# AdaLN transformer block: LN2's turned rows and three weight sets split in high and low fp32r parts; query and key buffers for three head groups instead of four

## The chip, the cores and the metric

The kernel is one launch on one core of one Trainium2 chip. The metric is the time of the whole launch in device microseconds. Before the change the median of three runs is 1087.39 us (1085.41 to 1090.95). The engines are TensorE (PE; its weight loads are a row of their own, PEld), VectorE (DVE), ScalarE (ACT), GpSimd (POOL) and SyncE (SP), which here only issues transfers.

## The reference, cut to what matters

Batch 4, 1024 tokens, width 256, 16 heads of 16. An attention block is followed by a block with eight small autoencoders, of which the one with the least error picks an adapter for the batch.

```python
mod = (silu(c) @ wmod).reshape(4, 6, 1, 256)           # sa, ca, ga, sb, cb, gb; |ga|, |gb| at least 0.25
h = layernorm(x) * (1 + ca) + sa
q, k, v = split_heads(h @ qkv_w.T)                      # 16 heads of 16
x = x + ga * (softmax(q @ k.T / 4) @ v @ proj_w.T + proj_b)

h = layernorm(x) * (1 + cb) + sb                        # "LN2"; below: h2
base = h @ W_base + b_base                              # 256 x 256
hid  = relu(h @ W_enc[n] + b_enc[n])                    # n = 0..7, 256 x 64 each: together 256 x 512
recon = hid @ W_dec[n] + b_dec[n]
top1 = argmin_n mean((recon - h) ** 2)                  # one adapter for a batch of the block
mid  = relu(h @ W_down[top1] + b_down[top1])            # 256 x 64
x = x + gb * (base + mid @ W_up[top1] + b_up[top1])     # 64 x 256
```

All inputs and outputs are float32. (The FFN part of the reference names 16 batches of 256 tokens as its shape constants; with the arrays that come in, it runs on 4 batches of 1024.)

## The kernel before, in words

**Units.** The attention is cut into 256 units. A head group `gi` (0 to 15) is four heads of one batch; with a half `c` of 512 queries it makes a pass, 32 in all, in the order of the table `SEQ`. A pass has 8 units, one for each 128 keys. A unit is four score products `E` (one for each head; PE writes 128 keys x 512 queries in a bank `pE`, ACT takes its exponential into `P`, L1003), and one `PV`, which multiplies `P` with V into `pO`. The row maximum is needed first: `M` (1024 products, 32 for each pass) computes scores the other way round into `pM`, and DVE reduces them (L1124). The maxima are turned (`mturn`) and sent by DMA into two extra rows of the query operand `QO`. M runs at least 48 products ahead of E.

Both have room for four groups. A copy of group `gi` waits until the last E of group `gi - 4` has been read. `hi` and `lo` are one buffer: a group's ACT step waits until the group before has landed.

**The rest, for each batch.** `proj` (attention output), `bn2`, `ln2s`, `ln2n` (LN2's statistics and normalised rows X), `xturn` (PE turns X; ACT scales it into `h2T`, features on partitions, with the sum over tokens, L1086), `xsq` (ACT squares `h2T`, L1095), `enc` (8 tiles of 128 tokens x 512, each two fp32 products over halves of the 256 features; DVE takes the maximum into `Hb`, L1279), `gram` (`half` in the last batch), `pick`, `select` and `fetch` (the chosen adapter's weights come by four DMAs), `base` or, in batches 0 to 2, the base product inside `out`, `mid`, `out`. `prepb` on POOL scales W_base by gb into `wbg`.

**What sets the order.** `order()` writes one list of steps, and each engine runs its own part of it in that order. `plan()` gives due units; `before(s)` gives the steps that must lie some units back. A burst is 3 E and about 3 M, and then either one or two PV, or pieces of long steps; QUIET steps (work of ACT, DVE and POOL) and SHORT steps (transposes) follow a burst. When all M are out (unit 243), E goes on alone, with pieces between. After the last PV, the second half of the last batch's LN2, `enc`, `half`, `pick`, `select`, `fetch`, `base`, `mid` and `out` run one behind the other. PE waits for a bank before it writes in it: three `pM`, three `pE` and one `pX`.

L701 is the helper `mm`: all products with weights other than transposes have this line.

## Time and profile before

| | |
|---|---|
| median of 3 runs | 1087.39 us |
| profiled execution | 1087.94 us |
| its span | 1086.1 us |
| outside the span | 1.84 us |
| mean granted TensorE clock | 0.974 |
| PE, DVE, ACT, POOL busy | 95%, 73%, 59%, 17% |

A PE row of a product covers its fill and drain too, so that rows overlap and 95% busy isn't 95% of PE's peak. What a product costs is read from the distance between the starts of successive weight loads or products. An fp32 product appears as two records, an fp32r product as one. PEclk is the granted clock of TensorE as a share of its higher level. Rows of POOL are rough.

### The profile page before, as it was taken

Reading aid. Unit: us, or ns where it says so; the run is one execution under the profiler, and the core shown is the slowest. Engines: PE = TensorE matmul, PEld = TensorE weight load, DVE = VectorE, ACT = ScalarE, POOL = GpSimd, SP = SyncE. Lnnn points to the kernel's source line nnn. Section 1 sums busy time; section 2 is a strip of 40 time slices with the busy share of each in tenths; the row PEclk is TensorE's granted clock in tenths of the full one; section 3 lists DMA queues with packets and bytes.
Section 4 is the critical chain, followed back from the end, with each engine's and each line's share of the span. In section 5 each row is a group of like instructions: output and inputs, shape, how many; then the busy total and the mean of one; then the engine's idle time right before and its main releaser. Section 6 shows DMA issues by size and latency. Waiting matters only on the chain.

```text
span 1086.1 us, 15998 instructions
## 1 busy us (share of the span) xinstructions
PE 1032.0 (95%) x5824; PEld 496.9 (46%) x5824; DVE 795.4 (73%) x1565; ACT 644.1 (59%) x1261; POOL 180.3 (17%) x300
## 2 busy tenths in 40 slices
...
PEclk7979999999999999998999999999999998999988
...
GB/s 162 181 1 70 2 79 25 64 76 25 69 1 70 20 41 20 59 26 59 97 11 69 13 10 59 20 44 118 84 35 2 1 2 26 49 49 3 1 1 44
DMA packets 33218, 48.60 MB, mean 45 GB/s; under 512 B 6947, under 2 KB 25384, under 8 KB 33132
## 3 DMA queue, kind: packets, MB, share of 16 engines
...
## 4 chain that ended last, share of the span: by engine, by line
PE 85%; DVE 7%; ACT 5%; issue 2%; DMA 1%; SPq 0%; POOL 0%; ACTq 0%; DVEq 0%
PE pE L701 26%; PE pX L701 23%; PE pO L701 22%; PE pM L701 11%; DVE mx L1124 2%; ACT P L1003 1%; ACT h1T L1037 1%; ACT h2T L1086 1%; ACT hi L1053 1%; PE pX L760 1%; DVE Atok L1149 1%; DVE lo L1212 1%; DVE Hb L1279 1%; PE pX L826 0%; DVE junk L1263 0%
## 5 line engine op out<-in xcount | busy, mean ns | idle before, releaser
L1124 DVE TENSOR_REDUCE mx<-pM 128x1 f32<-128x512 f32 x1006 | 630.1, 681 | 117.7 <-PE pM L701 115.1
L1003 ACT ACTIVATE P<-pE 128x512 f32<-128x512 f32 x995 | 525.6, 599 | 245.2 <-PE pE L701 242.1
L701 PE MATMUL pM<-KO,QO 48*128 48x512 f32 x1006 | 368.8, 454 | 6.1 <-DVE mx L1124 3.7
L701 PE MATMUL pE<-QO,KO 50*128 50x512 f32 x995 | 349.1, 440 | 20.7 <-DVE Atok L1149 7.4
L701 PEld LDWEIGHTS pE<-QO,KO 50*128 50x128 f32 x995 | 164.2, 187 | 241.2 <-issue 134.6
L701 PE MATMUL pO<-P,V 128*17 128x512 f32 x2048 | 258.7, 603 | 1.0 <-ACT P L1003 1.0
L701 PEld LDWEIGHTS pM<-KO,QO 48*128 48x128 f32 x1006 | 163.8, 187 | 35.7 <-DVE mx L1124 23.9
L1442 POOL CAST mh<-mxc 128x16 fp32r<-128x16 f32 x32 | 6.4, 202 | 502.4 <-DVE mxc L1133 502.3
L701 PEld LDWEIGHTS pO<-P,V 128*17 128x17 f32 x2048 | 41.5, 96 | 102.8 <-issue 94.6
L701 PE MATMUL pX<-h1T,wqkv_s 128*128 128x512 f32 x112 | 60.9, 648 | 0.6
L701 PE MATMUL pX<-X,Hb 128*128 128x258 f32 x208 | 53.4, 395 | 0.7 <-DVE lo L1212 0.7
L701 PEld LDWEIGHTS pX<-X,Hb 128*128 128x128 f32 x208 | 37.0, 190 | 14.8 <-issue 8.9
L701 PE MATMUL pX<-wenc_s,h2T 128*128 128x512 f32 x72 | 39.6, 654 | 1.6 <-ACT h2T L1086 1.4
L1212 DVE SCALAR_TENSOR_TENSOR lo<-pX,cst,hi 128x512 fp32r<-128x512 f32 x28 | 21.0, 751 | 26.7 <-ACT hi L1053 26.6
L701 PE MATMUL pX<-Hb 128*128 128x128 f32 x224 | 31.6, 289 | 0.0
L701 PEld LDWEIGHTS pX<-Hb 128*128 128x128 f32 x224 | 28.9, 199 | 5.8 <-issue 5.2
L1053 ACT ACTIVATE hi<-pX,cst 128x512 fp32r<-128x512 f32 x28 | 19.2, 686 | 17.8 <-PE pX L701 17.5
L1501 POOL TENSOR_SCALAR X<-x,mv,rs 128x256 f32<-128x256 f32 x24 | 29.2, 1226 | 1.5 <-POOL rs L1491 0.5
L1406 POOL TENSOR_SCALAR xin<-xin,mv,rs 128x256 f32<-128x256 f32 x24 | 29.2, 1224 | 1.0
L701 PEld LDWEIGHTS pX<-h1T,wqkv_s 128*128 128x128 f32 x112 | 18.3, 193 | 20.6 <-issue 17.1
L1010 ACT ACTIVATE osb<-pO 128x512 f32<-128x512 f32 x32 | 19.2, 600 | 12.9 <-PE pO L701 12.6
L701 PE MATMUL pE<-wenc_s,h2T 128*128 128x512 f32 x52 | 24.3, 592 | 0.0
...
## 6 DMA issues: line engine op xcount, KB each, us to landing
KO<-hi SPq DMA_DIRECT2D x56, 128.0 KB, 4.0
QO<-hi SPq DMA_DIRECT2D x56, 128.0 KB, 5.8
...
KO<-lo SPq DMA_DIRECT2D x28, 128.0 KB, 3.8
QO<-lo SPq DMA_DIRECT2D x28, 128.0 KB, 6.3
...
```

The source lines that it names most:

```text
L701: return e.matmul(o, lhsT, rhs, start=start, stop=stop)
L760: a = e.transpose(o[:, 128 * k:128 * k + 128], osb[:, 128 * k:128 * k + 128], ident)
L1003: e.activation(P[:, u % 3, j, :], bank(s), ACT.Exp).then_inc(*empties(s))
L1010: e.activation(osb[:, :], pO[:, :], ACT.Copy).then_inc(s_osb, 1)
L1037: a = e.activation(h1T[:, c, 256 * k:256 * k + 256], bank(s)[:, 256 * c:256 * c + 256], ACT.Identity, bias=modT[:, c, b:b + 1], scale=modT ...
L1053: e.activation(halves(gi)[0][:, cs], bank(s), ACT.Identity, scale=qscale).then_inc(s_hi, 1)
L1086: e.activation(h2T[:, c, 512 * th:512 * th + 512], bank(s), ACT.Identity, bias=modT2[:, c, b:b + 1], scale=modT2[:, 2 + c, b:b + 1], accum ...
L1124: e.tensor_reduce(mx[:, hq % 2, k:k + 1, kh], bank(s), AX.X, ALU.max, negate=True).then_inc(*empties(s))
L1149: e.tensor_tensor(dst, v[:, :, :, 0:HD], rec[:, :, :].unsqueeze(3).to_broadcast([128, 4, 4, HD]), ALU.mult).then_inc(*empties(s))
L1212: e.scalar_tensor_tensor(out=lo_[:, cs], in0=bank(s), scalar=qscale, in1=hi_[:, cs].bitcast(F), op0=ALU.mult, op1=ALU.subtract).then_inc(* ...
L1406: a = e.tensor_scalar(xt[:, t, :], xt[:, t, :], mv1[:, k, t, 0:1], rs1[:, k, 1, t:t + 1], ALU.subtract, ALU.mult)
L1501: a = e.tensor_scalar(X[:, t, 0:D], x2[:, t, :], mv2[:, t, 0:1], rs2[:, 1, t:t + 1], ALU.subtract, ALU.mult)
```

## The change

1. `h2T` is gone. `xturn` writes into a buffer `h2f` with room for half the tokens; a new step `xhi` writes the high part `h2h` (ACT, a copy) and the low part `h2l` (POOL, a subtraction), both fp32r. In the last batch's second half both are done by DVE.
2. W_enc is split once by POOL into `weh` and `wel` (`wsplit`, unit 24); `wbg` for each batch into `wbh` and `wbl` (`prepb`); the chosen W_down into `wdh` and `wdl` (`fetch`: POOL, in the last batch DVE).
3. Each fp32 product in `enc`, `base`, the base part of `out`, and `mid` becomes three fp32r products (`thrice`): high x high, high x low, low x high.
4. To have room for this, `QO` and `KO` hold three groups instead of four. A copy of group `gi` waits for the last E of group `gi - 3`, and in the list it isn't put before that unit is over. The due units of `qk` move, `SEQ` takes the two halves of queries apart for the last three groups only, and the last batch's first half is due 7 units later.
5. `h2f` shares memory with W_enc as it is loaded, and the unsplit `wbg` with the squares of `xsq` (`junkx`), from which waits follow (`s_wen`, `s_wbg`, `s_xsq`, `s_hl`). `mid` waits for the split W_down alone and no longer for all four DMAs.

```diff
-SEQ = [(gi, c) for gi in range(4 * NB - 4) for c in range(2)]
-SEQ += [(4 * NB - 4 + g, c) for c in range(2) for g in range(4)]
+SEQ = [(gi, c) for gi in range(4 * NB - 3) for c in range(2)]
+SEQ += [(4 * NB - 3 + g, c) for c in range(2) for g in range(3)]
...
+    at(24, ("wsplit", 0), ("wsplit", 1))
     for gi in range(2, 4 * NB):
-        u = {2: 0, 3: 8, 13: 168, 14: 177, 15: 188}.get(gi, 16 * gi - 36)
+        u = {2: 0, 4 * NB - 1: 200}.get(gi, 16 * gi - 34)
...
-            halves = ((B - 30, (0, 1)), (B, (2, 3))) if q == LAST else ((B, (0, 1, 2, 3)),)
+            halves = ((B - 23, (0, 1)), (B, (2, 3))) if q == LAST else ((B, (0, 1, 2, 3)),)
...
-        return [(("ln1turn", b, 2 * a[1] + i), 1) for i in range(2)] + (
-            [(("qk", gi // 4, gi % 4, 1), 7)] if gi > 1 else [])
+        return [(("ln1turn", b, 2 * a[1] + i), 1) for i in range(2)] + [(("moved", 4 * b + a[0] - 1), 2)]
...
+            [(("xhi", b, a[0] - 2), 0), (("xsq", b, 0), 0)] if a[0] > 1 else [])
+    if kind == "xhi":
+        return [(("xturn", b, a[0]), 0.7)]
...
-        return [(("xturn", b, 2 * (a[0] // 4) + i), 1) for i in range(2)]
+        return [(("xhi", b, 2 * (a[0] // 4) + i), 1.5) for i in range(2)]
...
-        for _ in range(3):
-            if moving:
+        for _ in range(6 if moving and moving[0][1] == 4 * NB - 1 else 3):
+
+            if moving and (moving[0][1] < 3 or at >= 32 * (SEQ.index((moving[0][1] - 3, 1)) + 1)):
                 out.append(moving.popleft())
...
-        QO = sb("QO", [128, 2, 4, T], R)
-        KO = sb("KO", [128, 2, 4, T], R)
+        QO = sb("QO", [128, 3, 2, T], R)
+        KO = sb("KO", [128, 3, 2, T], R)
...
+        def split(b, k):
+
+            return (s_hL, k - 1) if b == LAST and k > 1 else (s_hl, 4 * b + k + 1)
+
+        def thrice(mm, o, xh, xl, wh, wl, start, stop):
+
+            mm(o, xh, wh, start, False)
+            mm(o, xh, wl, False, False)
+            return mm(o, xl, wh, False, stop)
...
-                        pe.wait_ge(d_w[6], 16)
+                        pe.wait_ge(s_wen, 2)
                         for c_ in range(2):
-                            pe.wait_ge(*emptied("xturn", b, 2 * (t // 4) + c_))
-                    a = mm(o, h2T[:, c, 128 * t:128 * t + 128], wenc_s[:, c, :], c == 0, c == 1)
+                            pe.wait_ge(*split(b, 2 * (t // 4) + c_))
+                    sl = slice(128 * t, 128 * t + 128)
+                    a = thrice(mm, o, h2h[:, c, sl], h2l[:, c, sl], weh[:, c, :], wel[:, c, :], c == 0, c == 1)
...
-                        pe.wait_ge(d_sel, 64 * (b + 1))
-                    a = mm(o[0:H, :], wdn[:, c, :], h2T[:, c, 512 * h:512 * h + 512], c == 0, c == 1)
+                        pe.wait_ge(*((s_wdL, 1) if b == LAST else (s_wdn, b + 1)))
+                    sl = slice(512 * h, 512 * h + 512)
+                    a = thrice(mm, o[0:H, :], wdh[:, c, :], wdl[:, c, :], h2h[:, c, sl], h2l[:, c, sl], c == 0, c == 1)
...
                         for c in range(2):
-                            mm(r, h2T[:, c, 128 * tt:128 * tt + 128], wbg[:, c, :], c == 0, False)
+                            thrice(mm, r, h2h[:, c, sl], h2l[:, c, sl], wbh[:, c, :], wbl[:, c, :], c == 0, False)
...
+                elif kind == "xhi" and not (s[1] == LAST and s[2] > 1):
+                    act.wait_ge(*(full("out", b - 1, 3) if b else landed(1)))
+                    act.wait_ge(*emptied("xturn", b, k))
+                    e.activation(h2h[:, c, 512 * th:512 * th + 512], h2f[:, c, :], ACT.Copy).then_inc(s_hh, 1)
...
+                elif kind == "xhi" and s[1] == LAST and s[2] > 1:
+                    e.tensor_copy(h2h[:, c, sl], h2f[:, c, :]).then_inc(*link.up())
+                    dve.wait_ge(*link.now())
+                    e.tensor_tensor(h2l[:, c, sl], h2f[:, c, :], h2h[:, c, sl].bitcast(F), ALU.subtract).then_inc(s_hL, 1)
+
+                elif s == ("fetch", LAST):
+                    dve.wait_ge(d_wdn, 16 * NB)
+                    e.tensor_copy(wdh[:, :, :], wdn[:, :, :]).then_inc(*link.up())
+                    dve.wait_ge(*link.now())
+                    e.tensor_tensor(wdl[:, :, :], wdn[:, :, :], wdh[:, :, :].bitcast(F), ALU.subtract).then_inc(s_wdL, 1)
...
+                elif kind == "xhi" and not (s[1] == LAST and s[2] > 1):
+                    pool.wait_ge(s_hh, nth[s])
+                    e.tensor_tensor(h2l[:, c, sl], h2f[:, c, :], h2h[:, c, sl].bitcast(F), ALU.subtract).then_inc(s_hl, 1)
...
-                    if gi >= 4:
-
-                        sp.wait_ge(*full("E", 8 * SEQ.index((gi - 4, 1)) + 7, 3))
+                    if gi >= 3:
+
+                        sp.wait_ge(*full("E", 8 * SEQ.index((gi - 3, 1)) + 7, 3))
```

**PE, behind the last PV: the second half of the last batch.** `cst,X` are the transposes of `xturn`, `X,Hb` belongs to `half`. Before:

```order
L859 MATMUL pE<-cst,X 128x128 [waits XL,free3]
L859 MATMUL pE<-cst,X 128x128 x3
L859 MATMUL pM<-cst,X 128x128 x4
L701 MATMUL pX<-wenc_s,h2T 128x512 [waits free1,free3]
L701 MATMUL pX<-wenc_s,h2T 128x512
L701 MATMUL pM<-wenc_s,h2T 128x512 x2
L701 MATMUL pE<-wenc_s,h2T 128x512 [waits free5]
```

PE at the same place, now:

```order
L886 MATMUL pE<-cst,X 128x128 [waits XL,free4]
L886 MATMUL pE<-cst,X 128x128 x3
L886 MATMUL pM<-cst,X 128x128 x4
L728 MATMUL pX<-weh,h2h 128x512 [waits hL]
L728 MATMUL pX<-wel,h2h 128x512
L728 MATMUL pX<-weh,h2l 128x512
L728 MATMUL pX<-weh,h2h 128x512
L728 MATMUL pX<-wel,h2h 128x512
L728 MATMUL pX<-weh,h2l 128x512
```

The order of the steps is the same; two products of a tile have become six, and the first waits for DVE's low part (`hL`) instead of ACT's write.

**DVE at that place,** where `junk,accA` ends the `half` before and `Hb` takes the `enc` results. Before:

```order
L1289 ISA accA 128x1
L1279 TENSOR_TENSOR Hb<-pX,nbe 128x512 [waits full6,free0]
L1279 TENSOR_TENSOR Hb<-pM,nbe 128x512 [waits full2]
L1279 TENSOR_TENSOR Hb<-pE,nbe 128x512 [waits full5]
L1279 TENSOR_TENSOR Hb<-pE,nbe 128x512 [waits full4]
```

DVE there, now:

```order
L1327 ISA accA 128x1
L1361 CAST h2h<-h2f 128x512 [waits free4,free2]
L1363 TENSOR_TENSOR h2l<-h2f,h2h 128x512 [waits vlink]
L1361 CAST h2h<-h2f 128x512 [waits free0]
L1363 TENSOR_TENSOR h2l<-h2f,h2h 128x512 [waits vlink]
L1317 TENSOR_TENSOR Hb<-pX,nbe 128x512 [waits full6]
```

Two casts and two subtractions have come in ahead of the first `Hb`.

**ACT in batch 1,** at the first two `xturn` (`P` is the exponential of E). Before:

```order
L1086 ACTIVATE h2T,xbar<-pX,modT 128x512 [waits full6,full2]
L1086 ACTIVATE h2T,xbar<-pE,modT 128x512 [waits full5]
L1003 ACTIVATE P<-pE 128x512 [waits full3]
L1003 ACTIVATE P<-pE 128x512 [waits full4]
L1003 ACTIVATE P<-pE 128x512 [waits full5]
L1003 ACTIVATE P<-pE 128x512 [waits full3]
```

ACT there, now:

```order
L1116 ACTIVATE h2f,xbar<-pX,modT 128x512 [waits full6,hl]
L1116 ACTIVATE h2f,xbar<-pE,modT 128x512 [waits full4,hl]
L1033 ACTIVATE P<-pE 128x512 [waits full5]
L1033 ACTIVATE P<-pE 128x512 [waits full3]
L1033 ACTIVATE P<-pE 128x512 [waits full4]
L1125 ACTIVATE h2h<-h2f 128x512 [waits free6]
L1125 ACTIVATE h2h<-h2f 128x512 [waits free4]
L1033 ACTIVATE P<-pE 128x512 [waits full5]
```

Two copies stand one burst behind the two writes of `h2f`, and these wait for POOL's low parts of the buffer's last content (`hl`).

**SP, the last group's copies.** `QO<-mT` are the maxima of a pass. In the list before, group 15's copies stand ahead of batch 2's last output stores and input loads:

```order
L1570 DMA KO<-hi 16x2x1024 [waits full4,free6]
L1570 DMA KO<-lo 16x2x1024
L1570 DMA KO<-hi 16x2x1024 x2
L1570 DMA KO<-lo 16x2x1024
L1570 DMA KO<-hi 16x2x1024
L1570 DMA QO<-hi 16x2x1024 x2
L1570 DMA QO<-lo 16x2x1024
L1570 DMA QO<-hi 16x2x1024 x2
L1570 DMA QO<-lo 16x2x1024
L1630 DMA out<-x 128x2x256 [waits free6]
```

SP there, now:

```order
L1662 DMA QO<-mT 2x4x128 [waits free2]
L1662 DMA QO<-mT 2x4x128 x3
L1653 DMA KO<-hi 16x2x1024 [waits full5,free6]
L1653 DMA KO<-lo 16x2x1024
L1653 DMA KO<-hi 16x2x1024 x2
L1653 DMA KO<-lo 16x2x1024
L1653 DMA KO<-hi 16x2x1024
L1653 DMA QO<-hi 16x2x1024 x2
L1653 DMA QO<-lo 16x2x1024
L1653 DMA QO<-hi 16x2x1024 x2
L1653 DMA QO<-lo 16x2x1024
L1662 DMA QO<-mT 2x4x128 [waits free3]
```

They stand in units 208 and 209 now, behind the maxima of pass 26, and nothing but maxima follows. The first M of group 15 stands at the start of unit 212.

## Rows read from the trace of the kernel before

**Rows 1.** The page, part 1 and the granted clock of part 2.
```profile
PE 1032.0 (95%) x5824; PEld 496.9 (46%) x5824; DVE 795.4 (73%) x1565; ACT 644.1 (59%) x1261; POOL 180.3 (17%) x300
PEclk7979999999999999998999999999999998999988
```

**Rows 2.** The page, part 4: the chain that ended last.
```profile
PE 85%; DVE 7%; ACT 5%; issue 2%; DMA 1%; SPq 0%; POOL 0%; ACTq 0%; DVEq 0%
```

**Rows 3.** Windows of 40 us: length, busy us by engine, clock, DMA.
```profile
80.00:120.00 40.00, 39.78 (x231) 15.90 (x234) 36.73 (x66) 31.65 (x63) 4.54 (x10) 1.00 0.33 48
...
320.00:360.00 40.00, 38.19 (x196) 15.18 (x192) 31.13 (x58) 25.05 (x50) 8.49 (x13) 1.00 0.31 53
```

**Rows 4.** PE's groups by form: busy us, mean ns, idle before.
```profile
L701 PE MATMUL pM<-KO,QO 48*128 48x512 f32 x1006 | 368.8, 454 | 6.1 <-DVE mx L1124 3.7 <-DVE h2T L1212 1.1 <-ACT h2T L1086 0.5
L701 PE MATMUL pE<-wenc_s,h2T 128*128 128x512 f32 x52 | 24.3, 592 | 0.0
```

**Rows 5.** PE's weight loads in order of time: start, us, load.
```profile
1050.36 0.19 PEld L701 LDWEIGHTS pM<-wenc_s,h2T 128*128 128x128 f32 x1 [0.24 <-issue]
1050.79 0.19 PEld L701 LDWEIGHTS pM<-wenc_s,h2T 128*128 128x128 f32 x1 [0.24 <-issue]
...
1056.09 1.61 PEld L701 LDWEIGHTS pM<-X,Hb 128*128 128x128 f32 x8 [1.67 <-issue]
1057.72 1.07 PEld L701 LDWEIGHTS pM<-Hb 128*128 128x128 f32 x8
1058.72 1.39 PEld L701 LDWEIGHTS pE<-X,Hb 128*128 128x128 f32 x7
```

**Rows 6.** The burst at 829 us, in order of time.
```profile
828.11 0.50 PE L701 MATMUL pE<-QO,KO 50*128 50x512 f32 x1
828.71 1.57 ACT L1003 ACTIVATE P<-pE 128x512 f32<-128x512 f32 x3 [1.45 <-PE pE L701]
828.75 1.89 DVE L1124 TENSOR_REDUCE mx<-pM 128x1 f32<-128x512 f32 x3 [1.47 <-PE pM L701]
829.01 0.30 PEld L701 LDWEIGHTS pX<-wenc_s,h2T 128*128 128x128 f32 x2 [0.37 <-issue]
...
831.78 0.18 PEld L701 LDWEIGHTS pE<-QO,KO 50*128 50x128 f32 x1 [0.76 <-issue]
```

**Rows 7.** Groups by form on ACT, POOL and DVE.
```profile
L1010 ACT ACTIVATE osb<-pO 128x512 f32<-128x512 f32 x32 | 19.2, 600 | 12.9 <-PE pO L701 12.6
...
L1470 POOL TENSOR_TENSOR wbg<-wb_s,bc 128x512 f32<-128x512 f32 x4 | 5.2, 1291 | 0.0
...
L1279 DVE TENSOR_TENSOR Hb<-pX,nbe 128x512 f32<-128x512 f32 x18 | 12.3, 685 | 14.6 <-PE pX L701 14.6
```

**Rows 8.** A one-input DVE pass over 128x512 in SBUF, in order of time.
```profile
71.71 0.41 DVE L1250 TENSOR_SCALAR nbe<-nbe 128x512 f32<-128x512 f32 x1
```

**Rows 9.** The end of the last batch, in order of time.
```profile
1045.62 0.77 ACT L1086 ACTIVATE h2T<-pM,modT 128x512 f32<-128x512 f32 x1
...
1046.62 3.47 PE L701 MATMUL pX<-wenc_s,h2T 128*128 128x512 f32 x4 [1.37 <-ACT h2T L1086]
...
1075.46 1.90 PE L701 MATMUL pM<-h2T,wdn 128*64 128x512 f32 x4 [1.08 <-DMA wug<-in_bup]
...
1079.01 1.13 PE L701 MATMUL pM<-wug,mid 65*128 65x256 f32 x4
```

**Rows 10.** POOL behind the maxima of passes 26 and 27.
```profile
827.34 0.20 POOL L1442 CAST mh<-mxc 128x16 fp32r<-128x16 f32 x1 [10.06 <-DVE mxc L1133]
...
861.19 0.20 POOL L1442 CAST mh<-mxc 128x16 fp32r<-128x16 f32 x1 [33.20 <-DVE mxc L1133]
```

**Rows 11.** SP's queue: a group's first and last copy.
```profile
774.25 0.60 SPq L1570 DMA_DIRECT2D KO<-hi  x1
...
781.25 0.59 SPq L1570 DMA_DIRECT2D QO<-lo  x1
```

**Rows 12.** The page, part 6: KB each, median us to landing.
```profile
QO<-lo SPq DMA_DIRECT2D x28, 128.0 KB, 6.3
```

More of the change, by code:

```diff
@@ L33 @@
 SHORT = {"ln1turn", "mturn", "oturn", "atturn", "xturn", "select", "modT2"}
-QUIET = {"gates", "ln1load", "ln1s", "ln1n", "prep", "prepb", "xload", "addx", "bn2", "ln2s", "ln2n", "xsq", "wload", "scale", "pick", "fetch"}
+QUIET = {"gates", "ln1load", "ln1s", "ln1n", "prep", "prepb", "xload", "addx", "bn2", "ln2s", "ln2n", "xsq", "xhi", "wsplit", "wload", "scale", "pick", "fetch"}
 BURST = 3
@@ L76, in plan @@
                     at(u, ("proj", q, k), ("bn2", q, k), ("ln2s", q, k), ("ln2n", q, k))
-                    at(u, ("xturn", q, k))
+                    at(u, ("xturn", q, k), ("xhi", q, k))
                 for th in sorted({k // 2 for k in ks}):
@@ L154, in before @@
     if kind == "xturn":
-        return [(("ln2n", b, 2 * (a[0] // 2) + i), 1.5) for i in range(2)]
+        return [(("ln2n", b, 2 * (a[0] // 2) + i), 1.5) for i in range(2)] + (
+            [(("xhi", b, a[0] - 2), 0), (("xsq", b, 0), 0)] if a[0] > 1 else [])
+    if kind == "xhi":
+        return [(("xturn", b, a[0]), 0.7)]
+    if kind == "wsplit":
+        return []
     if kind == "enc":
-        return [(("xturn", b, 2 * (a[0] // 4) + i), 1) for i in range(2)]
+        return [(("xhi", b, 2 * (a[0] // 4) + i), 1.5) for i in range(2)]
     if kind == "gram":
@@ L162, in before @@
     if kind == "base":
-        return [(("xturn", b, 2 * (a[0] // 2) + i), 1) for i in range(2)] + [(("prepb", b), 1)]
+        return [(("xhi", b, 2 * (a[0] // 2) + i), 1.5) for i in range(2)] + [(("prepb", b), 2)]
     if kind == "xsq":
-        return [(("xturn", b, 2 * a[0] + c), 1) for c in range(2)]
+        return [(("prepb", b), 0)] + [(("xturn", b, 2 * a[0] + c), 1) for c in range(2)]
     if kind == "pick":
@@ L218, in order @@
     done = {("ln1turn", 0, k): -9 for k in range(4)}
-    done["gates", 8] = -9
+    done["gates", 8] = done["moved", 1] = -9
     def come(u):
@@ L402, in order @@
     fill(len(spare) - 2)
-    now(("xturn", q, 2), ("xturn", q, 3), ("xsq", q, 0), ("xsq", q, 1), *(("enc", q, t) for t in range(4, 8)))
+    now(("xturn", q, 2), ("xturn", q, 3), ("xhi", q, 2), ("xhi", q, 3), ("xsq", q, 1), *(("enc", q, t) for t in range(4, 8)))
     now(*(("half", q, p, 1) for p in range(4)), ("pick", q), ("select", q), ("fetch", q))
@@ L509, in adaln_block @@
         h1T = sb("h1T", [128, 2, T])
-        h2T = sb("h2T", [128, 2, T])
+        h2f = sb("h2f", [128, 2, 512])
+        h2h = sb("h2h", [128, 2, T], R)
+        h2l = sb("h2l", [128, 2, T], R)
         x2 = sb("x2", [128, 8, D])
```

102 lines of the change are left out of this document (71 added, 31 removed).

## The prediction

> **What bounds the kernel now.** First the page: PE is busy 95% of the span, DVE 73%, ACT 59%, POOL 17% [rows 1]. Busy rows of PE overlap, so 95% alone proves nothing. The chain of waits does: 85% of the time that it follows back from the end is PE's own, 7% DVE's, 5% ACT's [rows 2]. The windows tell the stages apart. From 80 to 120 us, without LN2 work, DVE is busy 36.7 of 40 us and is as much a bound as PE; from 320 to 360 us, where batch 0's encoder runs, PE is at 38.2, DVE at 31.1 and ACT at 25.1, and POOL has 31 us free [rows 3]. The work that is changed lies in stages of the second kind. One burst there shows it in order of time: it begins at 828.11, 3 E and 3 M take until 829.01, then three encoder pieces, and the next burst's first load is at 831.78. That is 3.67 us of PE, against 1.57 us of ACT for the exponentials and 1.89 us of DVE for the maxima, plus one `Hb` of 0.69 [rows 6, 7]. What is taken from PE there shortens the burst.
>
> **What a product costs.** The weight loads of one encoder tile start at 1050.36 and 1050.79 [rows 5]: 0.43 us for a record. A tile's fp32 product has two records, 0.86 us, so with its two halves of the features a tile costs 1.72 us. The trace has no fp32r product with 128 rows of weights, but E and M are fp32r: one record each, M's of 454 ns where an fp32 record of equal columns has 592 [rows 4]. The burst bounds it: its six products of 512 columns take 0.90 us [rows 6]. They use 48 or 50 of the 128 rows, so two can run side by side, but at 0.43 a product even three pairs would need 1.29. So an fp32r product streams its columns once where an fp32 record does it twice, and I take half of 0.43, 0.215, for a one-pass product of 512 columns.
>
> For 256 columns one pass would stream in 0.107 (a quarter of the 0.43). There the weight load may end later than the stream. The nearest rows: eight records with 128-wide weights and 128 columns, loads starting at 1057.72 and the next group at 1058.72, so 0.125 each; eight with 258 columns between 1056.09 and 1057.72, 0.204 each [rows 5]. Lower bound 0.107; upper bound 0.204, if one pass saved nothing. I take 0.125, the row in which the load and not the stream counts.
>
> The Trainium skill speaks against this. By "TensorE: Matmul & The Clock Gate", section "The mechanism", a weight load overlaps products in flight only where they use other row groups of the array. All these products use all rows. By that rule each one-pass product would pay its load too, and three of them would cost more than one fp32 product. The trace doesn't agree for two-pass records; for one pass nothing here shows it, and it is the fourth rival below.
>
> **The sum, on PE, in the loop.** 28 of the 32 encoder tiles lie in the loop (the other four are in the tail): 1.72 less 6 x 0.215 = 1.29, 0.43 each: 12.0 us. `mid` has two products of 512 columns in each half, so again 1.72 against 1.29: six halves in batches 0 to 2, 2.6 us. The base products have 256 columns: 16 for each of three batches, 32 records at 0.21 = 6.7 us against 48 x 0.125 = 6.0, so 0.7 each; the last batch's first two banks 0.4 more. Together 2.5 us (bounds: 5.5 gained at 0.107, 10.8 lost at 0.204). All of it: 17.1 us.
>
> How much of it is time? The chain's share of PE is 85%; some encoder pieces stand in bursts where DVE (1.89 for maxima, 0.69 for `Hb`, statistics of the next LN1) ends just as late. I take 80%: 13.7 us. Bounds: 100%, 17.1, and 40%, 7.
>
> **What is added.** ACT: 14 copies of 128x512 in the loop. The nearest row is the copy out of `pO`, 0.60 us [rows 7]: 8.4 us of ACT. They stand in pairs, one burst behind the two `h2f`, and a burst with a pair has 1.57 + 1.20 = 2.8 us of ACT. A burst of PE with pieces or PV takes 2.5 to 3.7, so most is covered, but ACT isn't idle just before. I take 0.4 for a pair, 2.8 us in all (bounds 0 and 8.4).
>
> POOL: 14 subtractions, four splits of `wbg`, one of W_enc, three of W_down. At 1.29 for 128x512 with two inputs [rows 7] the subtractions are 18 us, the rest, taken at the same rate, some 18, in an engine that is busy 180 of 1086. They cost nothing while they are done before `enc` and the next `xturn` ask: between `xhi` of the first pair and the second `xturn` lie 2 to 4 units of over 4 us (passes 26 and 27 are 33.85 us apart for 8 units [rows 10]), and POOL has 6 to 7 us of work ahead there (one `ln2n` of 2.4, its statistics, two subtractions). Cost 0; if the cover fails it is the third rival. The wait of `xsq` for the split `wbg` and that of ACT for `s_wen` are satisfied units ahead: 0.
>
> Three groups instead of four: for groups 3 to 14 the copies may start 11 or more units before M needs them, and twelve copies take 774.25 to 781.84, 7.6 us [rows 11], and 6.3 to landing [rows 12]. Only group 15 is near. It starts behind the last E of unit 207 and must have landed at the start of unit 212: 13.9 us are needed, 4 units are 16.9 before the change and about 15.5 after. Nothing stands ahead of it in SP's queue but maxima that are already out. Cost 0, with 1.6 us of room; I keep 3 us as an upper bound.
>
> **The tail.** Before, the second write of `h2T` begins at 1045.62 (0.77), and the encoder starts at 1046.62 [rows 9]. Now DVE casts (0.41 for one input in SBUF [rows 8]) and subtracts (0.69 [rows 7]) twice; the first pair runs beside ACT's second write, the second begins at about 1046.9. So the encoder starts at about 1048.1, 1.5 us later. The first four of its records took 3.47 us with their drain, the lower clock level (the last of PEclk's digits fell to 8 [rows 1]); then 0.43 each. Before: 1046.6 to 1055.1. Now 24 one-pass products, the first eight at the lower level in the same 3.3 us, 16 x 0.215 = 3.4: 1048.1 to 1054.8, 0.3 earlier. At the end `mid` waited for the last of four transfers and began at 1075.46, `out` at 1079.01 [rows 9]. Now it waits for the first one and for a cast and a subtraction on DVE (0.5 us for a quarter of the width): about 1074.7. Its two halves take 2.6 instead of 3.4, `out` starts at about 1077.6: 1.4 earlier. The tail gives 1.7 us; bounds -1 (the base products before `mid` come out later at the lower clock) and 3.
>
> **Sum.** 1087.94 of the profiled execution (span 1086.1, 1.84 around it) less 13.7, plus 2.8, less 1.7: 1075.3. The median of the runs is 0.55 below the profiled execution, which gives 1074.8; I forecast 1075.5. The order of the steps before unit 200 hardly moves, which I leave at 0 with 3 us to either side. Range of this case 1068 to 1082.
>
> **Rivals.**
> 1. *DVE takes over.* Encoder bursts get shorter, but DVE must still do the same maxima and `Hb`. For it: in the window with the encoder, DVE has 31.1 of 40 us, and at 80 to 120 us 36.7 [rows 3]. Against: 3.67 against 2.6 in the burst above. If only 40% of the 17.1 is kept, and ACT's copies cost 4: 1087.9 - 7 + 4 - 1 = 1084.
> 2. *More is gained.* All 17.1, copies covered, and 256 columns at 0.107 (3.0 more), tail 3: 1087.9 - 23.1 = 1065. For it: where PE is the bound it is so by a wide margin, and shorter products free banks earlier.
> 3. *ACT stands behind POOL.* The second pair of `h2f` waits for the low parts of the first, and with ACT the exponentials, the banks and PE stand still. For it: POOL takes its steps in order, and an `ln2n` (2.4 us) or a wait for statistics may stand ahead. If it comes in all four batches with 5 us, and the encoder waits as long once more for the second pair's low parts: 1075.5 + 4 x 5 = 1095.5, slower. It decides from about 3 us a batch. Against: 8 us or more of time for 6 to 7 of work.
> 4. *The weight load is not covered in one pass.* A record's load lasts 0.19 [rows 5]; its part beyond the fixed one is at least the 0.107 of 128 columns at the observed rate. One-pass products then cost 0.32 and 0.21: a tile 1.93 instead of 1.72, 256 columns 48 x 0.21 = 10.1 instead of 6.7. In the loop 34 x 0.2 + 3 x 3.4 + 2 = 19 us lost, 85% of it 16, copies 3: 1107, slower. Against: the transposes and the 128-column records run at 0.125 with 128-wide loads, so the load there is beside the product before it.
> 5. *The clock.* PE gets 5% less dense. PEclk is 9 and more through the loop, with one digit of 8 in the middle [rows 1]. A few more such drops would cost 1 to 2 us each; taken into the ranges, not a case of its own.
>
> **Chances.** Forecast 62%, rival 1 14%, rival 2 12%, rival 3 7%, rival 4 5%. The range that holds 8 in 10: 1066 to 1084. Half a percent, what a measurement of this kernel can tell from no change, is 5.4 us: faster means below 1082. Faster: 62 + 12 + a fourth of rival 1, 78%. Same: most of rival 1 and a little of rival 3, 13%. Slower 9%.
>
> **What would show it.** The weight loads of `weh` and `wel` about 0.215 us apart, those of `wbh` about 0.125; PE's group sums for them by that. A unit in the encoder's stages near 4.0 us instead of 4.2. In the tail, encoder start 2.5 us behind the start of ACT's second write, and 3.1 us between the first product of `mid` and the first of `out`. Wrong: starts 0.3 apart (rival 4); ACT idle with DVE's or POOL's low parts as releaser (rival 3); M waiting for QO's transfers at group 15; a DVE share of the chain well above 7% (rival 1).

## The result and the profile after

The changed kernel takes 1071.05 us (median of four runs, 1070.55 to 1072.19); the kernel before, 1088.91 beside it (four runs, 1085.41 to 1090.95). The ratio is 0.9841, 95% interval 0.9811 to 0.9871: 17.9 us gained, where 12 were forecast (1.5 of the 5.9 between them are the kernel before, which stood at 1087.39 when the forecast was made). The time lies within the forecast range, 4.5 us below the point. Two runs on record lie far from all others, at a much lower mean clock, one of the kernel before beside e1 (1242.96 us at 0.743) and one of e3 (1148.21 at 0.835), and all ratios leave them out.

The page of the changed kernel, parts 1, 2 and 4, answers to [rows 1, 2]:

```profile
span 1070.3 us, 16349 instructions
...
PE 1012.9 (95%) x5968; PEld 509.2 (48%) x5968; DVE 795.3 (74%) x1571; ACT 651.4 (61%) x1275; POOL 210.1 (20%) x332
...
PEclk7969999999999999999999999999999999999989
...
PE 83%; DVE 7%; ACT 6%; issue 2%; DMA 1%; SPq 0%; POOL 0%; ACTq 0%; DVEq 0%
```

PE has 19.1 us less of busy rows, POOL 30 us more, ACT 7.3 more, and the chain is nearly the same: still PE's. The digit of 8 in the middle of PEclk is gone, and the third digit has fallen from 7 to 6. The section on the experiments comes back to this.

The windows answer to [rows 3] (columns as there: length, PE, PEld, DVE, ACT, POOL, clock, DMA share, GB/s):

```profile
80.00:120.00 40.00, 39.79 (x232) 15.82 (x234) 36.75 (x66) 31.65 (x63) 4.55 (x10) 1.00 0.33 48
320.00:360.00 40.00, 37.10 (x219) 17.92 (x212) 30.82 (x57) 27.04 (x55) 12.10 (x15) 1.00 0.30 54
```

In the stage with the encoder PE has gone from 38.19 to 37.10 us of 40 and DVE has not risen (31.13, 30.82): PE leaves more gaps, and no other engine has become full in this window.

PE's weight loads of the last batch, in order of time, give the price of a one-pass product directly; they answer to [rows 5]. First the encoder's:

```profile
1037.15 0.19 PEld L728 LDWEIGHTS pE<-weh,h2h 128*128 128x128 f32 x1
1037.38 0.19 PEld L728 LDWEIGHTS pE<-wel,h2h 128*128 128x128 f32 x1
1037.60 0.19 PEld L728 LDWEIGHTS pE<-weh,h2l 128*128 128x128 f32 x1
1037.83 0.19 PEld L728 LDWEIGHTS pE<-weh,h2h 128*128 128x128 f32 x1
...
1038.98 0.19 PEld L728 LDWEIGHTS pE<-weh,h2l 128*128 128x128 f32 x1
```

Eight steps, from the first line to the last, take 1.83 us: 0.23 for 512 columns. And the base products, 256 columns, from the same view:

```profile
1053.32 0.19 PEld L728 LDWEIGHTS pE<-wbh,h2h 128*128 128x128 f32 x1
1053.43 0.19 PEld L728 LDWEIGHTS pE<-wbl,h2h 128*128 128x128 f32 x1
1053.55 0.19 PEld L728 LDWEIGHTS pE<-wbh,h2l 128*128 128x128 f32 x1
...
1054.37 0.19 PEld L728 LDWEIGHTS pE<-wbh,h2h 128*128 128x128 f32 x1
```

Nine steps in 1.05: 0.117 each, although the load's own row is 0.19 long. So a load of all 128 rows lies almost wholly beside the product ahead of it, in one-pass products too.

POOL's casts behind the maxima of passes 26 and 27, in order of time, answer to [rows 10]:

```profile
819.04 0.20 POOL L1497 CAST mh<-mxc 128x16 fp32r<-128x16 f32 x1 [6.81 <-DVE mxc L1171]
...
849.97 0.20 POOL L1497 CAST mh<-mxc 128x16 fp32r<-128x16 f32 x1 [30.28 <-DVE mxc L1171]
```

Eight units take 30.9 us where they took 33.9: 3.9 a unit, with 4.0 forecast. A third of that isn't the products' doing: in e1 below, which has the new list and the old products, the same two casts start at 826.99 and 859.91, 32.9 apart.

The tail of the changed kernel in order of time answers to [rows 9]:

```profile
1029.26 0.77 ACT L1116 ACTIVATE h2f<-pM,modT 128x512 f32<-128x512 f32 x1
...
1030.53 0.42 DVE L1361 CAST h2h<-h2f 128x512 fp32r<-128x512 f32 x1
...
1030.98 0.69 DVE L1363 TENSOR_TENSOR h2l<-h2f,h2h 128x512 fp32r<-128x512 f32 x1
...
1031.82 0.77 PE L728 MATMUL pX<-weh,h2h 128*128 128x512 f32 x1 [3.00 <-DVE h2l L1363]
1032.39 0.63 PE L728 MATMUL pX<-wel,h2h 128*128 128x512 f32 x1
1032.81 0.63 PE L728 MATMUL pX<-weh,h2l 128*128 128x512 f32 x1
...
1036.22 0.39 PE L728 MATMUL pM<-wel,h2h 128*128 128x512 f32 x1
1036.45 0.39 PE L728 MATMUL pM<-weh,h2l 128*128 128x512 f32 x1
```

The encoder starts 2.56 us behind the start of ACT's second write, as worked out (2.5). The steps of 0.42 until 1035.8 are TensorE's lower level; behind them the step is 0.23.

What stands ahead of the tail's transposes, from the first product of PV unit 255 to the first of them, before and then now:

```profile
1030.41:1044.19 13.78, 10.16 (x49) 7.73 (x49) 5.46 (x17) 1.19 (x2) 1.95 (x4) 0.88 0.00 0
```

```profile
1015.67:1027.76 12.09, 8.48 (x48) 6.50 (x49) 5.45 (x17) 1.19 (x2) 1.96 (x4) 1.00 0.00 0
```

The change doesn't touch this stretch. It is 1.7 us shorter because the granted clock is 1.00 in it and no longer 0.88: in e3 and e4 below, which have a low stretch there again, it takes 13.8 us.

### The profile page after: what moved, and what is told of

The parts are those of the page before. It is cut to its first block, busy times and chain, and to the rows that moved or that the text cites. A ratio compares the mean times of both kernels' runs of the same rounds, so it can differ in the third digit from the quotient of the medians.

```text
span 1070.3 us, 16349 instructions
## 1 busy us (share of the span) xinstructions
PE 1012.9 (95%) x5968; PEld 509.2 (48%) x5968; DVE 795.3 (74%) x1571; ACT 651.4 (61%) x1275; POOL 210.1 (20%) x332
## 4 chain that ended last, share of the span: by engine, by line
PE 83%; DVE 7%; ACT 6%; issue 2%; DMA 1%; SPq 0%; POOL 0%; ACTq 0%; DVEq 0%
PE pE L728 25%; PE pO L728 22%; PE pX L728 22%; PE pM L728 11%; ACT P L1033 2%; DVE mx L1162 2%; ACT h1T L1067 1%; ACT hi L1083 1%; ACT h2f L1116 1%; DVE Atok L1187 1%; DVE Hb L1317 1%; DVE lo L1250 1%; PE pX L787 1%; DVE x L1259 0%; DVE rec L1181 0%
## 5 line engine op out<-in xcount | busy, mean ns | idle before, releaser
L1566 POOL TENSOR_SCALAR rs<-mv 128x2 f32<-128x2 f32 x16 | 3.7, 231 | 103.7 <-DVE mv L1272 103.7
L1548 POOL TENSOR_TENSOR h2l<-h2f,h2h 128x512 fp32r<-128x512 f32 x14 | 17.7, 1283 | 30.4 <-ACT h2h L1125 30.4
```

The lines of the kernel that those rows point to most:

```text
L1548: e.tensor_tensor(h2l[:, c, sl], h2f[:, c, :], h2h[:, c, sl].bitcast(F), ALU.subtract).then_inc(s_hl, 1)
```

## The experiments

Four theories were at stake: that the gain is PE's time in the products (A), that a good part comes from the new list of steps and the rings of three groups (B), what ACT's copies cost, and, after the first runs, what the granted clock has to do with the tail (C: PE's standing still brings the lower level; D: the level falls whatever stands in PE's waits).

**How the runs are compared.** The runs come in three sets, each with the kernel before beside it: e1 to e4 (its median there 1091.91 us), e5 to e8 (1088.89), e9 to e11 (1088.57). So medians of different sets are compared by their ratios, and an absolute time that an expectation names can be off by 3 us for that reason alone. Runs of one kernel differ by up to 12 us, and the clock goes with most of it: the kernel before took 1097.5 at a mean of 0.968 and 1086.5 at 0.985. But at one mean clock, 0.974, it took 1088.0 and 1094.0. So two numbers are used: the ratio to the kernel before, and from each profile the *loop*, from the first product of PV unit 8 to that of unit 255, less what was lost at the lower level (granted clock in windows of 2.5 us, one minus it times the length, summed where it is under 0.97). This second number takes lost clock as lost time, which is right only where PE is the bound, and it comes from one profile of each variant. Five profiles whose loop does the same work bear it out: the changed kernel twice, and three of the variants below, give 915.4, 915.6, 916.0, 914.6 and 915.1. The windows of the loop and of the tail, first of the kernel before, then of the changed kernel:

```profile
95.02:1030.41 935.39, 908.56 (x5300) 428.66 (x5298) 708.59 (x1360) 604.10 (x1187) 152.22 (x249) 0.99 0.23 40
1030.41:1086.10 55.69, 43.80 (x190) 30.36 (x190) 18.30 (x62) 5.52 (x12) 3.39 (x6) 0.89 0.07 22
```

```profile
95.17:1015.67 920.50, 893.42 (x5424) 439.64 (x5422) 706.62 (x1360) 611.41 (x1201) 183.72 (x281) 0.99 0.22 41
1015.67:1070.30 54.63, 39.67 (x210) 31.67 (x210) 20.80 (x68) 5.52 (x12) 3.40 (x6) 0.91 0.07 22
```

Of 935.4 the kernel before loses 6.8 to the clock, the changed one 5.1 of 920.5: 928.6 and 915.4. So 13.2 us of the gain in the profile is less time in the loop, 1.7 a low stretch that didn't come, 1.1 the tail, where another low stretch of 1.7 didn't come, the one shown above.

**List and rings alone** (e1, and once more as e11). The kernel before with the changed kernel's list, due times and rings:

```
-QO = sb("QO", [128, 2, 4, T], R)
+QO = sb("QO", [128, 3, 2, T], R)
 ...
-        u = {2: 0, 3: 8, 13: 168, 14: 177, 15: 188}.get(gi, 16 * gi - 36)
+        u = {2: 0, 4 * NB - 1: 200}.get(gi, 16 * gi - 34)
 ...                       # the rest of the list's changes too; engine code of before
```

> The kernel before (1088.9) with the changed kernel's list of steps, due times and rings of three groups for the queries and keys (the steps xhi and wsplit stand in the list, empty), but with the fp32 products, the buffer h2T and all of the engine code of before. Theory A (the gain of 17.9 us is time of PE in the products, from 1.72 to 1.37 us an encoder tile, and the list adds next to nothing): within 2 us of before, 1087 to 1091. Rival B (a good part of the gain is the new list or the rings, since batch 0's encoder, PV units 72 to 92, took 78.9 us before and 78.6 after although it has 2.8 us less of products): 5 to 8 us faster than before, 1081 to 1084, most of it between units 92 and 160. I hold B's halfway point for likeliest: 1085.

Measured: 1085.89 (twelve runs), 0.9951 of before (0.9923 to 0.998): 5.3 us by the ratio, between the theories. The profile showed far less, so it was run again:

> Once more the kernel before with the changed kernel's list and three-group rings alone. In the first run it stood at 0.9951 of before with a mean clock of 0.977 against 0.975, while its profile, from PV unit 8 to the end and without the clock's low stretches, takes as long as that of before to 0.1 us. If the list gives nothing, 0.997 to 1.002 of before here; if it gives 3 us or more, 0.992 to 0.997 again.

Measured: 1088.34 (twelve runs), 0.9987 (0.9966 to 1.0008). The loops, e1 first:

```profile
98.02:1028.79 930.77, 906.30 (x5300) 427.61 (x5298) 706.97 (x1360) 604.20 (x1187) 152.25 (x249) 1.00 0.22 40
```

```profile
97.54:1032.57 935.03, 910.63 (x5301) 428.94 (x5299) 707.18 (x1360) 604.29 (x1187) 152.22 (x249) 0.99 0.22 40
```

The clock took 3.4 and 8.5 of them: 927.4 and 926.5, against 928.6 of before. The same program differs by 4.3 us in its loop from one run to the other, and 5.1 lie in the clock. List and rings give 1 to 2 us in the loop, not 5 to 8, and the ratios (5.3 and 1.4 us, the second not clear of 0) don't bear out B's 5 to 8 the second time: B falls. Their tails are even longer than that of before (57.1 and 56.9 us, where it has 55.7), with more of the lower level on the encoder and `mid`. B's first reason has an answer too. With the clock taken out in the same way, units 72 to 92 take 78.9 us before, 79.9 in e1, 80.0 in e11 and 78.6 in the changed kernel: the list alone costs 1.0 us there, and the products give 1.3. My own guess of 1085 was drawn from a comparison of two profiles by PV units, in which the kernel before has a low stretch at 507 us and the changed one has none. Here are its windows; the same stretch without it would be 3.4 us shorter, and that was the "gain" I had seen between units 116 and 160:

```profile
505.00:507.50 2.50, 1.51 (x4) 0.44 (x4) 2.37 (x9) 1.05 (x2) 0.81 (x1) 0.89 0.02 6
507.50:510.00 2.50, 2.50 (x9) 1.19 (x13) 2.50 (x5) 1.19 (x2) 2.42 (x3) 0.50 0.00 1
510.00:512.50 2.50, 2.50 (x16) 0.34 (x8) 0.18 (x1) 0.00 (x0) 2.50 (x4) 0.50 0.02 7
512.50:515.00 2.50, 2.50 (x12) 1.13 (x8) 1.42 (x3) 1.46 (x3) 0.06 (x1) 0.74 0.00 0
```

**One product less, one more** (e2, e3). In each half of an encoder tile:

```
 e2:  mm(o, xh, wh, start, False)              e3:  mm(o, xh, wh, start, False)
      return mm(o, xl, wh, False, stop)             mm(o, xh, wl, False, False)
                                                    mm(o, xl, wl, False, False)
                                                    return mm(o, xl, wh, False, stop)
```

e2 leaves a term of the encoder's sum out, the high part of the rows by the low part of W_enc.

> The changed kernel (1071) with two of the three one-pass products in each half of an encoder tile; high part of the rows times low part of W_enc is left out. PE has 0.456 us less for each of the 32 tiles, 14.6 us in all, and nothing else is changed. Theory A (PE is the bound in these bursts): 80 to 100% of it comes back, 1056 to 1059. Rival B (other engines end nearly as late, so the products gave less and the list gave the rest): 40 to 60%, 1062 to 1065.

Measured: 1064.35 (four runs), 0.974 (0.9693 to 0.9786).

> The changed kernel with a fourth one-pass product (low part times low part) in each half of an encoder tile: 14.6 us more on PE, nothing else changed. Theory A: 80 to 100% of it is seen, 1083 to 1086. Rival B: 40 to 60%, 1077 to 1080. If the two slopes differ, the longer products cost more than the shorter ones bring.

Measured: 1087.96 (ten runs, with the outlier), 0.9955 (0.9922 to 0.9989). Against the changed kernel that is -11.0 and +12.4 us by the ratios with 0.9841 as its own, of 14.6 us of PE: 75% and 85%. With its second ratio of 0.9852 (e5 below) it is -12.2 and +11.2, 84% and 77%. The intervals are some 4 to 5 us to either side, so the ratios show that both effects are there and can't tell one slope from the other. The loops can; e2 first:

```profile
100.61:1011.13 910.52, 880.04 (x5368) 429.64 (x5367) 705.26 (x1360) 610.83 (x1201) 183.51 (x281) 1.00 0.23 41
```

```profile
93.92:1027.52 933.60, 907.52 (x5480) 450.52 (x5479) 707.12 (x1360) 611.51 (x1201) 183.23 (x281) 0.99 0.22 40
```

Less the clock's 1.7 and 8.4 they are 908.8 and 925.2, and the 28 tiles of the loop have 28 x 2 x 0.23 = 12.9 us less or more of PE. So the shorter side gives 6.6 (51%), the longer costs 9.8 (76%): by the loop e2 lies in B's range of 40 to 60%, e3 a little below A's 80 to 100. The stages tell why. Below is the time between the first products of two PV units with the clock taken out: the change against the changed kernel (mean of seven profiles whose loop does that work or has the casts on POOL; they differ by 0.3 us at most in these stages), and in brackets its share of the PE time that e2 and e3 take or add.

| stage | encoder tiles | DVE busy, changed kernel | e2 | e3 |
|---|---|---|---|---|
| units 72 to 96, batch 0 | 8 | 80% | -1.2 (34%) | +2.1 (57%) |
| units 136 to 160, batch 1 | 8 | 79% | -1.8 (49%) | +3.3 (91%) |
| units 196 to 216, batch 2 | 8 | 73% | -2.1 (57%) | +3.3 (90%) |
| units 236 to 248, batch 3 | 4 | 53% | -1.8 (97%) | +1.8 (100%) |

Between these stages no difference is over 0.5 us. So one share for the whole loop is an average: in the last stage, where M runs out, DVE is busy half the time and all of a product's time is the kernel's; in batch 0, where DVE is at 80%, it is a third of a saving. There other engines end nearly as late: in e2 PE waits 5.3 us for DVE's `Hb` before it writes in `pE`, in the changed kernel 2.4, and DVE's part of the chain rises from 7 to 9% (page of e2, part 4):

```profile
PE 82%; DVE 9%; ACT 6%; issue 2%; DMA 1%; SPq 0%; POOL 0%; ACTq 0%; DVEq 0%
```

What the prediction's first rival names, DVE ending as late as PE, begins to show here, one product further on.

**ACT's copies: onto POOL, and twice** (e4, e6).

```
 e4, POOL:  pool.wait_ge(*emptied("xturn", b, k))
            e.tensor_copy(h2h[:, c, sl], h2f[:, c, :]).then_inc(*link.up())
            pool.wait_ge(*link.now())                  # then POOL's subtraction as before
                                                       # ACT's copy, and POOL's wait for it, go
 e6, ACT:   e.activation(h2h[...], h2f[:, c, :], ACT.Copy).then_inc(s_hh, 1)
           +act.wait_ge(s_hh, 2 * nth[s] - 1)
           +e.activation(h2h[...], h2f[:, c, :], ACT.Copy).then_inc(s_hh, 1)
     POOL: waits for the second copy before it subtracts
```

> The changed kernel with the high parts of the 14 halves in the loop written by POOL (a cast, then its subtraction) instead of ACT. ACT loses 14 copies of 0.6 us, 8.4 us; POOL gets 14 casts, some 10 to 15 us. Theory A (the copies cost 0.4 us a pair as forecast): 2 to 3 us faster, 1068 to 1069. Rival B (the copies are fully covered): the same, 1071. Rival C (POOL's low parts become late and ACT's next h2f waits for them): slower by 3 us or more, 1074 and up, with ACT idle behind POOL.

Measured: 1074.08 (six runs), 0.9855 (0.9816 to 0.9895). The time alone would fit rival C's "1074 and up", but the kernel before is 3 us slower in this set than in the first comparison, and the ratio is that of the changed kernel. The trace has no wait of ACT for POOL, and only one of PE, 0.3 us. The low parts weren't late: POOL's cast of 128x512 took 0.61 us, less than the 0.7 to 1.1 that I had allowed it.

> The changed kernel with each of ACT's 14 copies to the high part done twice, one behind the other: 14 x 0.6 = 8.4 us more of ACT in the encoder's stages, and POOL's low part later by 0.6 each. Theory A of the forecast (0.4 us for a pair of copies): the second set costs at least what the first does, 2.8 us, so 1074 or more. Rival (ACT is covered, the copies cost nothing, as the profile without them suggests with 1.8 us less of span and unchanged medians): within 1.5 us of the changed kernel.

Measured: 1073.88 (five runs), 0.986 (0.9836 to 0.9885), against 0.9852 of the changed kernel in the same set. The loops less the clock: 915.1 for e4 (918.46 less 3.4) and 919.6 for e6 (922.99 less 3.4), against 915.4. Moving the first set off ACT gives nothing; a second set costs 4 us in the profile, of which 1.3, 0.8, 0.9 and 0.6 lie in the four stages of the table above, and under 1 by the ratios, whose intervals of some 2.6 us to either side don't exclude 4. So the copies as they stand are covered, within about a microsecond, and the cover ends somewhere above one copy.

**The changed kernel again** (e5).

> The changed kernel once more, unchanged, beside the three variants that follow and the kernel before, since the runs of a kernel differ by several us and the mean granted clock of the run goes with that (before: 1097.5 at 0.968, 1086.5 at 0.985). Expected: 0.983 to 0.986 of before. In the profile the clock's low stretches should lie where they lay (72, 715, 907, 1030, 1062 us); what a low stretch costs is 1.7 us or twice that. If another one comes or goes, one profile says nothing about differences of 3 us.

Measured: 1073.17 (six runs), 0.9852 (0.9824 to 0.9879). Its low stretches did not lie where expected: that at 715 us is gone, one at 505 has come (length, PE, PEld, DVE, ACT, POOL, clock, DMA share, GB/s, as in all windows here):

```profile
505.00:510.00 5.00, 5.00 (x20) 1.94 (x19) 3.93 (x8) 2.56 (x5) 4.93 (x5) 0.66 0.02 5
510.00:515.00 5.00, 5.00 (x22) 1.62 (x24) 1.57 (x3) 2.01 (x5) 4.45 (x6) 0.66 0.00 0
```

The first profile of the same kernel has 1.00 there. So the program alone doesn't set where these stretches lie.

**The tail: another order, and filled gaps** (e7, e8).

```
 e7, DVE:  e.tensor_copy(h2h[:, c, sl], h2f[:, c, :]).then_inc(s_hH, 1)
          +for c in range(2) if c else ():             # both casts first
               dve.wait_ge(s_hH, c + 1)
               e.tensor_tensor(h2l[:, c, sl], ..., ALU.subtract).then_inc(s_hL, 1)
     PE:   high-part products of both halves of a tile, then its two low-part products
 e8, PE:  +keep({("xturn", LAST, 2): 8, ("enc", LAST, 4): 9,
          +      ("half", LAST, 0, 1): 3, ("mid", LAST, 0): 8}.get(s, 0) if piece == 0 else 0)
           # keep(n): n times mm(pO, h2h[:, 0, 0:128], weh[:, 0, :])
```

> The changed kernel with another order in the tail. DVE casts both halves to their high parts first and subtracts after that; PE runs the high-part products of tile 4 of the last batch behind the casts, and its low-part products last. PE should start the encoder at about 1030.6 instead of 1031.8, and wait a little for the low parts inside of the first tile: 0.5 to 1.2 us less, of a time of 1071. If the clock is at its low level there, the four high products take 1.7 us and hide the subtractions wholly: 1.2. Rival: nothing, since the first tile's end is set by the low parts, 1032.4 at best against 1033.9.

Measured: 1070.02 (six runs), 0.9837 (0.9803 to 0.9871). In its profile PE starts the encoder at 1029.18, 2.2 us behind the first of its transposes instead of 4.1, and the first Gram product at 1038.37, 11.4 behind them instead of 12.7: 1.3 us, a little more than expected. The tail as a whole is 2.9 us shorter, 51.69 instead of 54.63:

```profile
1014.91:1066.60 51.69, 40.27 (x210) 32.62 (x210) 20.71 (x68) 5.53 (x12) 3.42 (x6) 0.89 0.07 23
```

Another 1.3 of it is chance, not the new order. The second low stretch came at 1051.7, on the base products, and not at 1060, on `mid`. From the first base product to the first of `mid` it is 5.54 us with 1.7 lost to the clock in it and 5.56 in the changed kernel with nothing lost, since `mid` waits for DVE's low part of W_down; from `mid` to `out` it is 2.80 instead of 4.11. In e6, which has the old order, that stretch lies on the base products too, and `mid` to `out` is 2.74.

> The changed kernel with one-pass products that nobody reads (W_enc's high part by the rows' high part into the bank of the last PV) where PE stands still in the tail: 8 ahead of the third xturn (2.1 us idle), 9 ahead of the encoder (3.0), 3 ahead of the first half (0.9), 8 ahead of mid (2.5). At 0.228 they fit into the waits. Theory C (PE's standing still ahead of it is what brings TensorE to the lower level at 1029 and at 1060 us): the level stays at the upper one, the tail's 5.1 us lost to the clock come back, 1066 to 1068. Rival D (the level falls whatever stands in the gaps): 1071, or up to 3 us more, as products at the lower level take 0.425 and spill over.

Measured: 1071.45 (five runs), 0.9827 (0.9802 to 0.9851). The windows of the tail, of the changed kernel and then of e8:

```profile
1025.00:1030.00 5.00, 1.71 (x14) 1.31 (x13) 3.13 (x14) 1.51 (x4) 1.14 (x3) 0.94 0.00 0
1030.00:1035.00 5.00, 3.18 (x8) 2.54 (x9) 1.88 (x4) 1.45 (x6) 0.00 (x0) 0.50 0.00 0
1035.00:1040.00 5.00, 4.60 (x18) 3.38 (x16) 2.20 (x4) 0.00 (x0) 0.00 (x0) 0.88 0.00 0
...
1060.00:1065.00 5.00, 5.00 (x17) 3.37 (x16) 0.69 (x1) 1.36 (x2) 1.22 (x2) 0.66 0.00 0
```

```profile
1025.00:1030.00 5.00, 4.31 (x24) 3.65 (x22) 2.74 (x8) 0.60 (x1) 0.91 (x2) 1.00 0.00 0
1030.00:1035.00 5.00, 4.72 (x28) 3.81 (x28) 3.13 (x13) 1.60 (x5) 1.04 (x3) 1.00 0.00 0
1035.00:1040.00 5.00, 4.08 (x18) 3.06 (x17) 2.43 (x5) 1.36 (x5) 0.00 (x0) 1.00 0.00 0
1040.00:1060.00 20.00, 18.25 (x121) 16.00 (x120) 7.33 (x35) 0.00 (x0) 0.00 (x0) 1.00 0.00 1
1060.00:1071.70 11.70, 7.60 (x34) 5.23 (x32) 4.49 (x8) 1.37 (x2) 1.46 (x2) 1.00 0.32 101
```

The clock is at its upper level through the whole tail, which takes 51.12 us instead of 54.63. C holds, D falls: where PE stood still 2.1 and 3.0 us, the level fell, and with products in the gaps it doesn't. In e9 and e10 below the level stays up as well until 1062. Those are three tails of three with filled waits; all ten without them, those of before, e1 and e11 among them, have low stretches that lose 5.1 to 7.6 us. But 5.1 us of clock brought back only 3.5 us of time, since a part of the tail waits for other engines: 1.2 of the 5.1 lay in PE's own wait between the transposes and the encoder, which is 4.06 us long in both. By the ratios it is 2.7 (0.9827 against 0.9852), and the intervals overlap; in this profile more low stretches lie in the loop (8.5 us lost there against 5.1).

**All three together** (e9; e10 without the casts on POOL), with four of the products that nobody reads ahead of tile 4 instead of nine, and five more ahead of `select`.

> The changed kernel with three edits at once: POOL casts the 14 high parts of the loop, the tail's order (casts first, low-part products last), and PE's waits of the tail filled with products that nobody reads (8 ahead of the third xturn, 4 ahead of tile 4, 3 ahead of the first half, 5 ahead of select, 8 ahead of mid). Span without the clock's low stretches: 2.0 less by the first, 1.1 by the second; the third keeps the upper level in the tail, 3.4 to 5.1. Together 6 to 8 us less than the changed kernel beside it (1073.2): 1065 to 1067. If the edits don't add up, or the low stretches come in the loop instead, 1069 to 1071.

Measured: 1068.2 (six runs), 0.9818 (0.9786 to 0.9849).

> The same without the first edit, ACT writes the high parts of the loop again: 2 us more than with it, 1067 to 1069, if the copies cost what the profile says (0.3 a pair); the same time if they are covered.

Measured: 1069.02 (five runs), 0.9815 (0.9783 to 0.9847). Loop and tail of e9, then of e10:

```profile
94.46:1016.39 921.93, 895.18 (x5424) 440.99 (x5422) 706.67 (x1360) 604.10 (x1187) 191.49 (x295) 0.99 0.23 41
1016.39:1066.50 50.11, 43.22 (x238) 33.89 (x238) 20.71 (x68) 5.52 (x12) 3.42 (x6) 0.98 0.08 24
```

```profile
95.37:1017.30 921.93, 894.89 (x5424) 440.43 (x5422) 706.66 (x1360) 611.33 (x1201) 183.26 (x281) 0.99 0.22 41
1017.30:1067.20 49.90, 43.22 (x238) 33.88 (x238) 20.71 (x68) 5.52 (x12) 3.42 (x6) 0.98 0.08 24
```

The loops are alike to the last digit, with 7.2 us of ACT's work in one that the other has on POOL: the copies are covered. The tail gives 4.5 us, less than the 6 to 8 expected of the three. Against e7, which has the order alone, the fills are worth 1.8 (49.90 in e10 against 51.69). This is the fastest version that leaves no product out, 2.5 to 3.7 us below the changed kernel by the ratios (0.9818 against 0.9841 and 0.9852). The intervals overlap, so the tail's windows, not the runs' times, are what shows it.

## Why the prediction was right, point by point

The mechanism was right: PE's time in the products is what the kernel gained by, and no rival came whole. The time lies between the forecast and rival 2 (1065), of which one part came, the copies that cost nothing. The sum is nearer than its terms, which partly cancel. The sizes:

- **A product costs 0.215 for 512 columns, 0.125 for 256.** 0.23 and 0.117. A tile is 1.38 instead of 1.29, so the loop's saving is 34 x 0.34 = 11.6 for tiles and `mid`, and 3.8 for the base products (three times 6.7 less 5.6, and 0.5 for the last batch's first banks): 15.4 us instead of 17.1.
- **80% of it becomes time.** From list and rings alone (927.0, mean of e1 and e11) to the changed kernel (915.4) the loop becomes 11.6 us shorter, with the copies' cost in it: 75% of 15.4, where the prediction had 13.7. The 80% was a guess from the chain's share. The runs give it a shape: on average 76% for one product more, 51% for one less, and by stages from 34% to 100%.
- **ACT's copies cost 2.8.** This term was mis-sized: about 0. I had argued that ACT isn't idle just before a pair of copies; PE's burst is long enough all the same. A cost put 2.8 too high here and a gain put 2.1 too high at the products cancel to 0.7, so the loop's net of 10.9 stood near the 11.6 by luck.
- **Waits for POOL's splits and low parts: 0.** Right. The waits named as signs (ACT behind the low parts, M behind QO's transfers at group 15) are not among those of the changed kernel (in e1 and e6 PE waits once for `QO<-lo`, 0.5 and 0.8 us), and POOL had room even for the casts.
- **List and rings: 0, 3 to either side.** 1 to 2 us faster in the loop.
- **The tail gives 1.7.** This term was wrong, and its 1.1 is luck. The 1.1 counts from PV unit 255, and 1.7 of it is the low stretch that the kernel before has ahead of the transposes. From the first transpose to the end, which is what the prediction summed, the changed kernel takes 42.5 us where the one before took 41.9: 0.6 longer. The encoder's start was right. But its products save less: the first Gram product stands 12.7 us behind the transposes instead of 11.9, where 0.3 less was forecast, since ten of the 24 run at 0.42, not eight, and the others at 0.23, not 0.215. `mid` starts 0.2 us earlier, not 0.8, after 2.47 us of waiting for DVE's low part of W_down, and it began 4.1 us before `out` instead of 3.1, since the level fell in the middle of its products; at the upper level (e7) it is 2.8.
- **The clock, left within the ranges.** The loop of before lost 1.7 us more to it than that of after, and the stretch ahead of the transposes 1.7 more again. These 3.4 are the two profiles' doing and not the change's. They and the list's 1.6 are what lifts the profile's gain of 15.8 over the 12.6 of the sum; the tail's term takes 2.3 of it away again.

Sum in the profiles: 1086.1 to 1070.3 is 15.8; 11.6 products with their copies, 1.6 list and rings, 1.7 clock in the loop, 1.1 tail (1.7 clock, less 0.6), less 0.1 at the start. The medians of the first comparison say 17.9, those of the second 15.7.

The rival of the uncovered weight load, which the rule of the Trainium skill ("TensorE: Matmul & The Clock Gate", section "The mechanism") brings, named steps of 0.32 and 0.21. The loads above stand 0.23 and 0.117 apart. By that rule a load overlaps products in flight only on other row groups; the trace doesn't agree, as all 128 rows are used by both. The same section also names a background weight buffer into which a load may go ahead of products in flight, and the trace doesn't speak against that.

## What to carry to other kernels

Three one-pass products in place of one fp32 product gain a fifth of PE's time at 512 columns (1.38 for 1.72) and a sixth at 256; look for it wherever PE ends most bursts, and ask how many more such steps it takes until the next engine ends them, since the first saving here was worth 75% of its PE time and the second 51%, a third in the stage where DVE is busiest and all of it where M has run out.

Before comparing two profiles stage by stage, take out the stretches at TensorE's lower level: one of them looks just like a gain of 3.4 us by whatever was changed there. In a tail, lost clock is lost time only where PE is what the rest waits for. Letting PE work on something in its waits kept the level up here and gave 3.5 us of 1071, and 1.8 where the tail's order had been mended first.

## What the runs showed of the chip beyond that

- TensorE's low stretches cost 1.7 or 3.4 us each in the loop. Ahead of some of them PE had stood still: 1.0 us before that at 507 of the kernel before, 1.25 at 916, 2.1 and 3.0 around that at 1029 of the changed kernel. But the last waits ahead of three others are 0.22 us (the changed kernel at 715), 0.50 (the same at 906) and 0.33 (e5 at 507). So in the tail filled waits keep the level up, and in the loop no wait that we found tells where it will fall. One lies between 905 and 927 in most profiles, but in neither e2 nor e6; others, at 258, 327, 505, 715, 800, come and go between profiles of one program or of programs that are alike there. What decides between coming and going wasn't found.
- A run's time follows its mean clock: a line through the runs of the kernel before gives 7.0, 4.4 and 5.8 us less for each 0.01 more in the three sets (22, 11 and 17 runs).
- POOL's one-input cast of 128x512 takes 0.61 us, its subtraction of two inputs 1.28; DVE's, 0.42 and 0.69.
